# FFN seams: the normalisation of the next tiles runs on VectorE ahead of the tile sums, and the attention tiles' statistics run inside the gate and up loop

## What is computed

```python
x = x + attn_a(layernorm(x), ...)
x = x + ffn(layernorm(x), wq_gate, s_gate, wq_up, s_up, wq_down, s_down)
x = x + attn_b(layernorm(x), W_q, W_k, W_v, W_o)
x = x + ffn(layernorm(x), ...)          # the same weights
# ffn(x): gate = silu(x @ Wg.T); up = x @ Wu.T; return (gate * up) @ Wd.T
# layernorm(x) = (x - mean) / sqrt(var + 1e-5), over the 512 features
```

## Time and profile before

| | us |
|---|---|
| median of 3 executions | 1017.73 (1017.63 to 1019.08) |
| the profiled execution, its own time | 1019.8 |
| its span, first to last instruction | 1018.1 |

### The profile page before, as it was taken

How to read it: one execution, slowest core, us unless ns; L and a number is a source line. 1 busy time by engine, 2 the same in 40 slices (tenths; PEclk the granted TensorE clock), 3 DMA queues, 4 the chain that set the end, 5 groups by cost and what they waited for, 6 DMA issues and landing times.

```text
span 1018.1 us, 12993 instructions
## 1 busy us (share of the span) xinstructions
PE 970.5 (95%) x4818; PEld 549.3 (54%) x4818; DVE 568.9 (56%) x1092; ACT 406.7 (40%) x790; POOL 427.2 (42%) x440
## 2 busy tenths in 40 slices
PE   7999999987999999998989999999998999999997
PEld 4888888876744444443444445545454444444443
DVE  7566747567467666654453334623365576666542
ACT  4332323335477634663222211322133566346630
POOL 5554435458437665555310000000024466655553
PEclk9999999999999999999999999999999999999999
DMA  9200200013030000000000000000000000010001
GB/s 330 97 1 1 114 1 1 1 42 125 11 114 1 1 1 1 1 1 1 1 1 1 1 1 1 1 1 1 1 1 1 1 1 1 32 52 1 1 22 62
DMA packets 12302, 26.05 MB, mean 26 GB/s; under 512 B 1744, under 2 KB 1744, under 8 KB 12240
## 3 DMA queue, kind: packets, MB, share of 16 engines
q1 hardware_dynamic: 12240, 25.22, 6.8%
HBM read 21.02 MB, written 4.19 MB: 25 GB/s over the span
## 4 chain that ended last, share of the span: by engine, by line
PE 79%; DVE 9%; POOL 4%; issue 3%; ACT 3%; DMA 1%; SPq 0%; POOLq 0%; DVEq 0%; ACTq 0%
PE psum L1745 51%; PE psum L1970 13%; PE psum L1972 12%; PE psum L2097 2%; PE psum L1778 1%; PE psum L1767 1%; POOL hid L756 1%; DMA wqk_raw<-wk 1%; DVE xres L1370 1%; DVE xq L1225 1%; DVE state L1357 1%; DVE xn L1202 1%; POOL xrstd L610 1%; DVE wv_lo L1256 1%; DVE ln_bn L1192 1%
## 5 line engine op out<-in xcount | busy, mean ns | idle before, releaser
L760 POOL TENSOR_TENSOR hid<-hid,hid_hi 128x512 f32<-128x512 f32 x88 | 102.0, 1159 | 93.6 <-DVE hid_hi L1499 93.6
L1970 PE MATMUL psum<-xf,w_gu 128*128 128x512 f16 x352 | 133.8, 380 | 0.0
L1970 PE MATMUL psum<-xf,w_s 128*128 128x512 f16 x264 | 100.0, 379 | 1.9 <-DVE up L1472 1.3
L1972 PE MATMUL psum<-xf,w_gu 128*128 128x512 f16 x264 | 100.1, 379 | 0.0
L789 POOL TENSOR_TENSOR yt<-yt,sd_rows 128x512 f32<-128x512 f32 x32 | 51.7, 1617 | 61.1 <-DVE yt L1549 61.1
L604 POOL TENSOR_TENSOR ln_rstd<-ln_var,minus_half 128x1 f32<-128x1 f32 x28 | 16.5, 594 | 140.1 <-DVE ln_var L1168 140.1
L610 POOL TENSOR_TENSOR xrstd<-xvar,minus_half 128x1 f32<-128x1 f32 x32 | 19.1, 600 | 124.6 <-DVE xvar L1196 124.6
L1012 ACT ACTIVATE hid_lo<-hid 128x512 f16<-128x512 f32 x88 | 54.9, 624 | 33.5 <-POOL hid L760 33.5
L756 POOL TENSOR_TENSOR hid<-up,gate 128x512 f32<-128x512 f32 x44 | 55.9, 1271 | 27.0 <-ACT gate L1007 27.0
L1972 PE MATMUL psum<-xq,w_s 128*128 128x512 f16 x176 | 66.7, 379 | 0.0
L1970 PEld LDWEIGHTS psum<-xf,w_gu 128*128 128x128 f16 x352 | 34.3, 97 | 54.1 <-ACT acc L997 15.5
(11 more groups left out here) (275 smaller groups left out, 2411.9 us busy)
## 6 DMA issues: line engine op xcount, KB each, us to landing
out<-xres SPq DMA_DIRECT2D x16, 256.0 KB, 2.0
xres<-x SPq DMA_DIRECT2D x3, 1024.0 KB, 13.5
codes_gu<-gateT SPq DMA_DIRECT2D x1, 2816.0 KB, 16.7
codes_gu<-upT SPq DMA_DIRECT2D x1, 2816.0 KB, 10.7
codes_da<-downT SPq DMA_DIRECT2D x1, 1536.0 KB, 6.9
codes_db<-downT SPq DMA_DIRECT2D x1, 1280.0 KB, 9.9
xres<-x SPq DMA_DIRECT2D x4, 256.0 KB, 3.0
wqk_raw<-wk SPq DMA_DIRECT2D x1, 1024.0 KB, 7.6
```

The lines of the kernel that those rows point to most:

```text
L760: nc.gpsimd.tensor_tensor(hid[:, :], hid[:, :], hid_part(hid_hi, j, half), ALU.subtract).then_inc(rest_done, 1)
L1970: nc.tensor.matmul(bank(use[0]), w, x_operand(piece, k, False), start=start and k == 0, stop=False, skip_group_check=not start)
L1972: last = nc.tensor.matmul(bank(use[0]), w, x_operand(piece, k, True), start=False, stop=k == 1, skip_group_check=not start)
```

## The change

The stretch of VectorE between loop and tile sums, and the statistics of the attention tiles, are put in another order. In F1,0 and F2,0 `x_normalise` of pair 0 stands ahead of all tile sums, and that of pair i + 1 right behind `x_second` of pair i. For pairs 1 and 3 that is the place they had; pair 2 moves from ahead of `yt(4)` to ahead of `yt(3)`. In F1,1 the statistics of the four tiles run in the passes j = 2 to 5 of the loop, POOL's `rstd` in the same passes; tiles 0 and 1 are normalised ahead of the tile sums, tiles 2 and 3 behind `split_lo` of tiles 0 and 1. The programs of TensorE, ACT and SP are unchanged, and so is the number of instructions.

```diff
@@ gpsimd, gate and up loop and tile sums
+                    if blk == 1 and 1 < j < 6:
+                        rstd(ln_n("FB", 0, j - 2), j - 2)
                     if b == 0 and j in (2, 4, 6, 8):
                         x_rstd(blk + 1, (j - 2) // 2)
                 for t in range(BT):
                     n = BT * blk + t
-                    if blk == 1 and t in X_AFTER:
-                        l = X_AFTER.index(t)
-                        rstd(ln_n("FB", 0, l), l % 4)
                     u.read_out(down_hi(t))
@@ vector, gate and up loop
                     if b == 0 and 1 < j < 10:
                         x_stats(blk + 1, j - 2)
+                    if blk == 1 and 1 < j < 6:
+                        if j == 2:
+                            dve.wait_ge(x_updated, updates(0, 7))
+                        stats("FB", 0, j - 2)
                     if j < JT:
                         gate_first(j)
@@ vector, tile sums
-                def x_before(t):
-
+                if b == 0:
+                    x_normalise(blk + 1, 0)
+                elif blk == 1:
+                    normalise("FB", 0, 0)
+                    normalise("FB", 0, 1)
+
+                def x_after(t):
                     if b == 0 and t in X_AFTER:
-                        x_normalise(blk + 1, X_AFTER.index(t))
+                        i = X_AFTER.index(t)
+                        x_second(blk + 1, i)
+                        if i < 3:
+                            x_normalise(blk + 1, i + 1)
                     if blk == 1 and t in X_AFTER:
                         l = X_AFTER.index(t)
-                        if l == 0:
-                            dve.wait_ge(x_updated, updates(0, 7))
-                        stats("FB", 0, l)
-                        normalise("FB", 0, l)
-
-                def x_after(t):
-                    if b == 0 and t in X_AFTER:
-                        x_second(blk + 1, X_AFTER.index(t))
-                    if blk == 1 and t in X_AFTER:
-                        split_lo("FB", 0, X_AFTER.index(t))
+                        split_lo("FB", 0, l)
+                        if l < 2:
+                            normalise("FB", 0, l + 2)
 
                 for t in range(BT):
                     n = BT * blk + t
-                    x_before(t)
                     u.full(down_hi(t))
```

## The result

| | before | changed |
|---|---|---|
| median of 7 executions, us | 1019.08 (1017.1 to 1020.63) | 1013.84 (1010.76 to 1015.94) |
| the profiled execution, own time / span | 1019.8 / 1018.1 | 1013.73 / 1012.0 |

A forecast was written before the change was run, and what follows sets the result against it. TensorE's work plus its gaps was taken as the bound. Gaps of 9.24 us less 2 x 0.24 at pair 1 gave 8.76 us, so 1017.73 became 1009.0 us; the whole range was 1007.9 to 1011.9.

The forecast's parts named there:

- The gap at the start of B: Start of layer B: the 2.3 us wait for `aT_lo` moves with TensorE's last down product and stays as it is.
- The gaps and their cause: Seams of F1,0, F1,1 and F2,0: TensorE loses 9.24 us waiting for VectorE's late normalisations, the most the change can give.
- Pair 0, pair 2 and tile 0 of F1,1: F1,0 and F2,0: pair 0's 2.48 and 2.47, pair 2's 0.42 and 0.41 us go; F1,1: tile 0's 3.46.
- Pair 1: Seams of F1,0 and F2,0: its normalisation is late next, making TensorE wait 0.24 us in each.
- The bound of 1.4: Pair 1 in the seams: the wait is 1.4 us if both its instructions run at 1.49 us, the worst price seen.
- Pairs behind pair 1: Seams of F1,0 and F2,0: the pairs' remaining steps are tied to the transposes and move forward with them.
- The next block's start: Behind the seams of F1,0 and F2,0: the next block's first matmuls wait only for pair 3; no loss counted.
- Statistics in the passes: F1,1 loop, passes 2 to 5: the four tiles' statistics cost TensorE nothing, as nine passes still take 55.20 us.
- The one at 12%: Rival at pair 1: both its instructions take 1.49 us, giving 1011.3 us; chance 12%.
- the gain of F1,1 was not swallowed there: Rival at B's start: the `aT_lo` chain does not move with TensorE, gain 5.3, time 1012.4 us; chance 4%.
- nothing beside `xn` held them: Rival: something beside `xn`, say a bank, holds pair 0's transposes, 1017.7 us at the extreme; chance 2%.
- the slower kernel: Rival: statistics do not fit in F1,1's passes, each tile exposed by 3.46 us, giving 1022.8 us; chance 3%.

The follow-up runs named there:

- each of its two parts alone: Kernel before with only the F1,1 part (statistics in passes, tiles 0 and 1 ahead): 0.9949; with only the F1,0 and F2,0 pair moves: 0.9971.
- pair 0 alone: Kernel before with only pair 0 normalised ahead of the tile sums, pair 2 and F1,1 as before: 1021.53 us in one execution.

## Why pair 1 is late

```diff
+ width = 1 if b == 0 and t == 1 else D
- nc.gpsimd.tensor_tensor(cols(yt, t % 2), cols(yt, t % 2), sd_rows[:, :], ALU.mult)
+ nc.gpsimd.tensor_tensor(cols(yt, t % 2)[:, 0:width], cols(yt, t % 2)[:, 0:width],
+                         sd_rows[:, 0:width], ALU.mult)
```

> The changed kernel, but GpSimd multiplies only one column of tile 1's sum in F1,0 and F2,0 (this leaves out 511 of 512 columns of that product, so tile 1 of each batch isn't scaled). Theory (VectorE's add of tile 0 stands behind GpSimd's product of tile 1, 1.74 us instead of 0.67): the add takes 0.65 to 0.75 us, pair 1 starts about 1.0 us sooner after the last down matmul of tile 1 than the 5.3 us of the changed kernel, and the two gaps at pair 1 (0.38 and 0.43) are gone or under 0.1 in all. Rival (the pair's own two instructions are slowed beside GpSimd's subtractions and that alone makes the gaps): the add stays at 1.7, and the gaps stay at 0.8 in all.

VectorE's timeline in the seam of F1,0:

```profile
362.81 0.69 DVE L1527 TENSOR_TENSOR xres<-xres,yt 128x512 f32<-128x512 f32 x1 [0.79 <-POOL yt L789]
...
364.55 1.71 DVE L1202 TENSOR_SCALAR xn<-xres,xmv,xrstd 128x512 f32<-128x512 f32 x2
```

The update is back at 0.69 us, and the first instruction of pair 1 starts 364.55 - 360.49 = 4.1 us after the end of tile 1's down products instead of 367.01 - 361.91 = 5.1. Both gaps are gone: the seams take 31.98 us, 0.87 less each. The pair's own two instructions take 1.71 together in both kernels, so they are not it. The cause is shown: GpSimd's product of tile 1 holds up VectorE's update of tile 0. In the changed kernel two of these products stand back to back:

```profile
362.93 2.49 POOL L788 TENSOR_TENSOR yt<-yt,sd_rows 128x512 f32<-128x512 f32 x2 [3.38 <-DVE yt L1552]
...
L788 POOL TENSOR_TENSOR yt<-yt,sd_rows x2: 1267/1268/1269, 362.9 to 364.2; 128x512 f32<-128x512 f32 x2
```

The update starts at 364.23, as the second product does, ends 1.74 later, and the product ends at 365.42. So the update seems to make no way for 1.2 us and then to run in some 0.55, an estimate from these three times. In the kernel before the same two met in the other order: the update started at 365.73 and took 0.67, and the product started 0.15 us behind it and was the longer one.

```profile
365.88 1.65 POOL L789 TENSOR_TENSOR yt<-yt,sd_rows 128x512 f32<-128x512 f32 x1 [0.96 <-DVE yt L1549]
```

So the same update took 1.74 us behind the start of the product and 0.67 just ahead of it. The forecast weighed a slow instruction beside GpSimd for the normalisation, 1.49 us; here it was the update that was slow.

The obvious repair is to use VectorE's idle time and to normalise pair 1 ahead of the update:

```diff
+ if b == 0 and t == 1:
+     for use in x_banks(blk + 1, 0)[2:]:
+         u.full(use)                      # both halves of pair 0 transposed
+     x_normalise(blk + 1, 1)
  if t > 0:
      add_y(t - 1)
  # and in x_after(1) this normalisation is left out
```

> The changed kernel, but pair 1 is normalised as soon as the transposes of pair 0 are done, ahead of the update of tile 0, in the time in which VectorE waited for GpSimd and stood behind it. Theory: pair 1 is ready over 1 us ahead of its transposes, the two gaps of 0.8 us in all are gone in F1,0 and F2,0, and each of these seams takes 32.0 to 32.1 us instead of 32.85; the next block's start loses the 0.8 to 1.0 us that it loses now, or up to 0.3 less, since the steps behind pair 1 move too. Rival (the chain of copies and subtractions of a pair sets the pace): pair 2 is waited for instead, and the seam stays over 32.6.

Here the rival came true. Pair 1 has no gap any more, but the seams take 32.87 and 32.86 us. TensorE's timeline:

```profile
382.24 0.66 PE L1785 MATMUL psum<-ident,xn 128*128 128x128 f32 x4 [0.23 <-DVE xn L1201]
383.11 0.66 PE L1785 MATMUL psum<-ident,xn 128*128 128x128 f32 x4 [0.21 <-DVE xn L1201]
```

That is pair 3, with the same 0.83 us. F1,1 takes 78.46 us and F2,1 112.92, so the next block's start loses no less than in the changed kernel. What may set it is read off VectorE: in the changed kernel `x_second` of pair 0 starts at 365.90 and the one of pair 1 at 373.22, 7.3 us later, while TensorE needs 4.75 + 0.87 = 5.6 for a tile and a pair. The repair had pushed `x_second` of pair 0 back from 365.90 - 361.91 = 4.0 to 364.75 - 360.23 = 4.5 us behind the end of tile 1's down products. So the next kernel starts this chain earlier, ahead of the update, and normalises pair 1 behind it:

```diff
+ first = b == 0 and t in (1, 4)
+ if first:
+     x_after(t)
  if t > 0:
      add_y(t - 1)
  if b == 0 and t - 1 in X_AFTER:
      x_34_low(blk + 1, X_AFTER.index(t - 1))
- x_after(t)
+ if not first:
+     x_after(t)
```

> The changed kernel, but in F1,0 and F2,0 the subtractions of pairs 0 and 2, and with them the normalisation of pairs 1 and 3, stand ahead of the update of the tile before. Nothing is left out. Theory, as it stands after the repair of pair 1 alone (there pair 3 was waited for 0.83 us instead, and the seam stayed at 32.87): each pair's chain, subtraction on VectorE, two on GpSimd, a copy on ScalarE, the low sum and the sum of the next tile, takes 7.3 us from pair 0 to pair 1, while TensorE takes 5.6, so the start of pair 0's subtraction sets where pair 3 is ready. Here it starts 1.4 to 1.7 us after the last down matmul of tile 1 instead of 4.0, pair 1 is still ready in time, and the seam takes 31.9 to 32.1 us with no gap at any pair. The loss at the start of the next block falls below 0.5 us. Rival (the chain's pace is set by GpSimd's products, not by where it starts): pair 3 is waited for again, 32.5 us or more.

```profile
361.71 0.42 DVE L1213 TENSOR_TENSOR x_mid_f<-psum,x_first_f 128x256 f32<-128x256 f32 x1
...
362.84 1.95 DVE L1201 TENSOR_SCALAR xn<-xres,xmv,xrstd 128x512 f32<-128x512 f32 x2
364.71 1.21 DVE L1526 TENSOR_TENSOR xres<-xres,yt 128x512 f32<-128x512 f32 x1
```

On VectorE `x_second` now starts 1.6 us behind the end of tile 1's down products (360.11), and the seams take 31.99 and 31.98 us with no gap at any pair. So the order of these steps on VectorE is what made pair 3 late. Two things were moved at once, though: also at t = 4 `x_second` of pair 2 now stands ahead of an update of 0.6 us. It starts 378.14 - 360.11 = 18.0 us behind tile 1's down products instead of 380.01 - 360.23 = 19.8 with pair 1 early, and the update accounts for 0.6 of these 1.75. With pair 1 early, pair 3 was normalised 383.06 - 360.23 = 22.8 us behind tile 1's down products, and TensorE wants its second half at 22.1. Without the 0.6 it would be 22.2, with the other 1.15 alone 21.7, so the earlier head of the chain should be what counts; that is an estimate from these numbers, and the two moves were not run apart. The second half of the expectation missed: F1,1 still takes 78.38 and F2,1 112.76, so the slow start of the next block does not go away with an earlier chain.

## Why the next block starts slowly

```diff
- add_y(BT - 1)                                  # tile 7, at the end of the tile sums
+ # F1,1 and F2,1, pass 0, behind gate_first(0):
+ dve.wait_ge(y_scaled, BT * blk + BT)           # blk: the block before
+ nc.vector.tensor_tensor(xs, xs, cols(yt, 1), ALU.add).then_inc(x_updated, 1)
```

> The changed kernel, but the update of tile 7 (the last of the tile sums of F1,0 and F2,0) is made by VectorE behind the first gate sum of the next block. Theory (TensorE waits at the start of the next block because VectorE stands in this update, which waits for GpSimd's last product): the first gate sum ends 1.8 us sooner, and the gaps of 0.46 and 0.44 us at 399.6 and 400.9 fall to under 0.1 each, so F1,1 takes 77.6 instead of 78.5 and F2,1's start loses nothing. Rival (the next block's start is held by its operands, the low parts of pair 3): the gaps stay.

```profile
395.69 0.68 DVE L1533 TENSOR_TENSOR xres<-xres,yt 128x512 f32<-128x512 f32 x1
396.29 0.68 DVE L1468 TENSOR_TENSOR gate<-psum,acc 128x512 f32<-128x512 f32 x1
397.53 0.69 DVE L1457 TENSOR_TENSOR xres<-xres,yt 128x512 f32<-128x512 f32 x1 [0.56 <-POOL yt L788]
```

The first gate sum of VectorE starts 396.29 - 394.03 = 2.3 us after the block's first matmul instead of 4.1, both gaps are gone, F1,1 takes 77.55 us and F2,1 111.87. What is left of F1,1's loss, 0.08, goes with the gap of 0.22 in pass j = 4, which is still there. The cause is shown: the last update, with its wait for GpSimd, stands ahead of the gate sum, and TensorE now comes early enough to wait for it.

The other end of the same chain, the sum of tile 7 standing behind the last subtraction of pair 3:

```diff
- if b == 0 and t - 1 in X_AFTER:
+ if b == 0 and t - 1 in X_AFTER[:3]:
      x_34_low(blk + 1, X_AFTER.index(t - 1))
+ if b == 0 and t == BT - 1:
+     x_34_low(blk + 1, 3)
```

> The changed kernel, but in F1,0 and F2,0 the last subtraction of pair 3 (1.75 us) stands behind the sum and the update of tiles 7 and 6 instead of ahead of them. Theory (the chain at the start of the next block is the sum of tile 7, GpSimd's product of it, the update of tile 7, the first gate sum): the sum of tile 7 comes 0.8 us sooner, at its down product, but the subtraction stands beside GpSimd's product and stretches, so the first gate sum comes 0 to 0.8 us sooner and the loss at the next start of 0.8 to 0.9 us falls to between 0 and 0.8. Rival (only the update's wait for GpSimd matters, not what stands ahead of the sum): no change, 0.8 to 0.9.

F1,1 takes 78.03 us and F2,1 112.35: 0.45 and 0.42 less than in the changed kernel. The first gap is gone, the second of 0.45 is still there. So both count, what stands ahead of the sum and what stands ahead of the gate sum.

## Repairs together

Pair 1 ahead of the update and the late update of tile 7 together:

> The changed kernel with both repairs: pair 1 ahead of the update of tile 0, and the update of tile 7 behind the next block's first gate sum. Theory: the seams of F1,0 and F2,0 take 32.0 us, F1,1 takes 77.6 (its statistics cost 0.15), F2,1's start loses nothing; against the kernel before 2 x 2.85 + 3.46 - 0.15 = 9.0 us, which is what was forecast for the change itself, so the time is 0.9905 to 0.9920 of before. Rival (something else is next, at pair 2 or 3): 7.5 us or less.

0.9919 (0.9901 to 0.9936). The interval holds both the forecast and the rival's 7.5 us; the stretches decide. The seams take 32.86 and 32.87 us (pair 3), F1,1 77.38 (the gap in pass j = 4 is absent here), F2,1 111.84. The gain is 2.01 + 0.09 + 3.45 + 1.98 + 0.10 = 7.6 us, so the rival came true. The same with `x_second` first instead:

> The first of these with the update of tile 7 behind the next block's first gate sum; all parts of the change kept, nothing at the start of layer B. Theory: both seams 32.0 us, F1,1 77.4 to 77.6, F2,1 as before, no loss left but the small one of the statistics: 2 x 2.87 + 3.46 = 9.2 us less than before, 0.9905 to 0.9920 of it. Rival: a third wait shows and the gain stays at the 7.5 us of the version before.

0.9904 (0.9889 to 0.9919), 1009.97 us beside 1019.62 of the kernel before. The seams take 31.98 us each, F1,1 77.55, F2,1 111.86: 2.89 - 0.08 + 3.46 + 2.87 + 0.08 = 9.2 us from the stretches. This is the gain that the gaps of the earlier trace rows had promised, and it needed both repairs.

The gap at the start of B (2.3 us in the earlier trace rows) did not change, as forecast. It was tried with the first pair of repairs, and then with the better one:

```diff
- stats 0, stats 1, normalise 0, normalise 1, query products 0 to 3   # start of B, b == 0
+ stats 0, query product 0, stats 1, query product 1,
+ normalise 0, normalise 1, query products 2, 3
```

> As the one before, and at the start of layer B VectorE subtracts the first two query products between the statistics of the first tiles instead of behind their normalisation. Theory (the gap of 2.46 us there is VectorE's order, not the data): the gap falls to 0.0 to 0.3 us and nothing behind it grows; 11.2 to 11.5 us under the kernel before, 0.9885 to 0.9900 of it. Rival (the gap is the time from TensorE's last down product to the update of tile 7, which nothing here shortens): the gap stays over 1.5 us.

0.9899 (0.988 to 0.9918). From the first matmul of B to the first transpose of a tile it takes 517.58 - 502.01 = 15.57 us, against 526.44 - 508.43 = 18.01 before: 2.44 us, all of the gap. It was VectorE's order. With the 7.6 from the other stretches this makes 10.1 us, not the 11.2 to 11.5 expected, for these counted the seams at 32.0 us.

> The one before with the query products' subtractions between the first statistics at the start of layer B, which took 2.45 us off that stage. Theory: 11.6 us under the kernel before, 0.988 to 0.990 of it. Rival: the stages trade with each other and it is no better than 0.990.

0.986 (0.9842 to 0.9878), 1005.7 us beside 1019.62: better than the 0.988 expected. The medians differ by 13.9 us, and the interval, 12.4 to 16.1, leaves out the 11.6 that the stretches give (9.2 and 2.4 more). The trace holds a further 1.7 us: layer B, from its first matmul to the first of F2,0, takes 281.4 us, where 285.5 less 2.4 makes 283.1, and the granted clock is 1.00 all through it (last section). Whether the new order at the start of B keeps the clock up in the other executions too is left open; two traces, this one and the one with the first pair of repairs, show it so.

## Why the prediction was wrong

Two steps failed: the span ahead of pair 1, which was too short, and the start of the next block, which was put at nothing. Term by term:

- **The gaps and their cause**: right. 9.24 us lie where they were read, and a kernel that closes all of them gains that much.
- **Pair 0, pair 2 and tile 0 of F1,1**: right in what they show. The transposes of pair 0 follow at once, pair 2 has no gap, the seam of F1,1 gives 3.46. Pair 2's move was credited with 0.42, by the gap it had; it was worth 1.86, for without it pair 0's gain goes lost there.
- **Pair 1**: the term was mis-sized. The wait was forecast at 0.24 us and is 0.88, counted up to the next down product. The step that failed is "From `add_y(0)` to the first instruction of pair 1 were 367.55 - 365.73 = 1.82 us": this span was copied from an arrangement in which the update had started ahead of GpSimd's next product, and 367.01 - 364.23 = 2.8 were measured, since the update took 1.74 us instead of 0.67 behind it. The product came first because the sums of tiles 0 and 1 now follow each other. The update's own start was 0.3 us earlier than allowed, 2.3 instead of 2.6 us behind tile 1's down products, which gave a part back. Two times 0.64 is 1.3 us. The bound of 1.4 held.
- **Pairs behind pair 1**: "move forward with them" was right only by luck in the changed kernel. On VectorE pair 1's `x_second` follows pair 0's after 7.3 us, against TensorE's 5.6, and a wait of 0.83 us showed at pair 3 as soon as pair 1 was repaired.
- **The next block's start**: missed altogether, 0.83 us in F2,1 and 0.86 in F1,1 without its statistics, 1.7 in all. The failing sentence is "the next block's first matmuls wait only for pair 3": operands were looked at, but not the banks that the first sums must free. Before, VectorE had stood idle for 0.38 us only ahead of the sum of tile 7; that was all the idle time there was ahead of it for TensorE coming earlier.
- **Statistics in the passes**: 0.15 to 0.19 us where nothing was forecast, and nothing in the traces with the first pair of repairs. The comparison with F2,0 was close, but F2,0 has the powers in pairs every second pass; whether that makes the difference isn't shown.
- **The sum**: 8.76 - 1.3 - 1.7 - 0.2 = 5.6, and 5.64 were measured.
- **The base**: the forecast stood on a median of 3 executions, 1017.73; over 7 it is 1019.08. Of the 4.8 us between 1009.0 and 1013.84, 1.35 come from this and 3.1 from the gain; the other 0.4 is scatter.
- **Rivals**: none came true as told. The one at 12%, 1011.3 us, had both instructions of pair 1 at 1.49 us; they took 1.71 together, 0.88 us was lost and not 1.4, and the update was the slow one. B's start moved with TensorE (18.01 us to the first transpose in both kernels), so the gain of F1,1 was not swallowed there; the transposes of pair 0 followed at once, so nothing beside `xn` held them; and the passes held but for 0.2 us, against the slower kernel.

## What to carry to other kernels

A gap that is closed makes the busiest engine arrive earlier at everything behind it: for each later meeting point, the idle time that the other engine had ahead of it is the reserve, and it must be subtracted before a gap is counted as gain; freed buffers are such meeting points as much as operands. A duration read beside a neighbour doesn't hold when the reordering changes which of the two starts first; here that was VectorE next to GpSimd, 0.67 us or 1.74 for the same update. Repairing the first late step may only show the next one, as pair 3 did here behind pair 1.

## What the runs showed of the hardware

In the seam of F1,0, GpSimd's product on 128x512 took 1.27 us when VectorE read from the sum banks and then stood still beside it (362.93 in the changed kernel), 1.27 again when it had started ahead of VectorE's update (364.2), and 1.50 to 1.72 in the kernel before, where normalisations, updates and subtractions of VectorE ran beside it. In the same seam of the two kernels the normalisation on VectorE took 0.54 to 1.49 us, the update 0.67 to 1.74, the long one when it started behind GpSimd's product.

A part of the scatter between executions is TensorE's clock. In layer B the stretch from 780 to 800 us ran at a mean granted clock of 0.91 in the kernel before and at 1.00 in the kernel with pair 1 early. The columns are the stretch, its length, TensorE's busy time with the number of matmuls, the granted clock, and two of the DMA:

```profile
780.00:800.00 20.00, 17.95 (x79) 0.91 0.00 0
```

```profile
780.00:800.00 20.00, 19.99 (x92) 1.00 0.00 0
```

Read us by us, the clock of the kernel before is 0.85 from 783 to 784 us, 0.50 in each of the three from 784 to 787, 0.94 from 787 to 788, and 1.00 in the rest of the stretch. Where it is 0.50, matmuls of 512 columns start 0.43 us apart (785.20, 785.62, 786.05); where it is 1.00 again, 0.22 (787.23, 787.44, 787.66). What is short of 1.00 adds up to 0.15 + 3 x 0.50 + 0.06 = 1.71 us, an estimate of the time lost; the times of layer B below put it at 1.7. What TensorE did ahead of it was the same in both: it had waited 0.9, 0.9 and 2.2 us at the last steps of B, from 776.9 to 783.5 in the one and from 770.3 to 776.9 in the other.

In the five kernels with 287.0 to 287.2 us in the list below, a second such stretch lies behind the wait at the start of B. The kernel with pair 0 alone has its own in the seam of F1,1, and the same seam is at 1.00 in the others. First the kernel with the small product, then the one with pair 0 alone:

```profile
500.00:520.00 20.00, 17.70 (x75) 0.91 0.00 1
```

```profile
470.00:490.00 20.00, 16.65 (x72) 0.91 0.00 0
```

That makes the 1.7 us by which this seam was longer there. From the first matmul of B to the first of F2,0 it takes:

- 283.8 us with no such stretch: pair 1 early, the low part of pair 3 behind tile 7's sum;
- 285.5 us with one: the kernel before, the changed kernel, each of its two parts alone, pair 0 alone;
- 287.0 to 287.2 us with two: the small product, the late update of tile 7, `x_second` first, and both pairs of repairs;
- 281.4 us with none and the new order at the start of B.

So it differs between executions of kernels whose code is the same in that layer, in steps of 1.7 us, and what sets it off stays open. It is a reason to take gains of a few us from stretches and not from one execution's total, and to look at the clock of a stretch before its length is compared.
